# Score products of a quantised attention on 32 rows instead of 128, for the second and third of each four

## The chip, the cores and the metric

The kernel runs on one core of a Trainium2 chip. Its time is in device microseconds (us), the median over several runs; a second figure, the span, goes from the first to the last instruction of one profiled execution. The engines are named as in the profile: PE (TensorE, matrix products; PEld is its weight load, which can lie under a product), DVE (VectorE), ACT (ScalarE), POOL (GpSimd) and SP (SyncE, which here starts the DMAs).

## The reference, cut to what matters

Six layers follow one another on a tensor x of 2 x 128 x 256: a cross attention with 2048 context rows per batch, a mixing layer, experts, a second cross attention with fake quantisation, a dilated attention and a feed-forward layer. The change lies in the fourth. Its 16 heads have 16 dimensions each; all 2 x 128 queries attend all 2 x 2048 keys:

```python
q = _fq_sym(q, axis=-1)
k = _fq_sym(k, axis=-1)
v = _fq_sym(v, axis=2)
attn = jnp.einsum('bhqd,bhkd->bhqk', q, k)
attn = jax.nn.softmax(attn.astype(jnp.float32), axis=-1)
attn = _fq_unsigned(attn, axis=-1)
out = jnp.einsum('bhqk,bhkd->bhqd', attn, v)
```

`_fq_sym` rounds to 127 steps of the largest absolute value, `_fq_unsigned` to 255 steps of the largest. So a row of scores must be known up to its maximum before its exponentials are rounded.

## The kernel before

The program is written by hand, engine by engine, with semaphores; nothing is scheduled for it. The order of each engine is the order of its code.

The quantised attention has 32 units u, one per batch b (0, 1) and head h (0 to 15). A unit has 128 queries and 4096 keys. Its scores are computed twice: a first pass, `pe_first`, in products n of 512 keys (`NB` = 8 per unit, 256 in all), of which DVE takes only the maximum (`dve_first`, tile tops, L1892); and a second pass, `pe_second`, in chunks q of 1024 keys (`NC` = 4 per unit), two products each, of which ACT makes the exponentials (`act_exponentials`, L1885, which writes into the tile that the trace calls cT). SP turns these by DMA (L1980), and PE multiplies them with the values (`attend`, L1908, 16 products of 16 columns after the first two chunks of each unit). All score products are recorded with line 1843, in `pe_scores`, and the trace calls their operands kT and v_space (qT lies in that space).

Four heads share a group of 128 rows: the rows of kT hold, for each group, 4 x 32 rows, 32 per head (16 dimensions in two parts). The queries of one head stand in `m.qT[:, b, group, r, :]`, where r = h mod 4; only rows 32r to 32r + 31 hold them, the other 96 are zeros that POOL writes beforehand.

A slot is one (u, q) of the loop in `pe_attention`: the two second-pass products of chunk q, then two first-pass products for a unit that lies one or two further on, then whatever the side program has due (small stages of the other layers for the other batch), and `attend`. For u = 1 to 31 there are 124 slots; the last six have no first-pass products left. First-pass products use PSUM banks 0, 1, 2 in turn (n % 3), and a product waits until DVE has read the bank (q_max). Second-pass products use banks 3 to 6 in two pairs and wait for ACT (q_exp). The first 20 first-pass products and the four chunks of unit 0 are issued earlier, by `drain` in `pe_cross`, between the products of the last units of the first cross attention (L1060, L1085, L1095, L1098, L1075, L1106, L1112):

```python
DRAIN = (0, 2, 2, 2, 3, 3, 2, 2, 1, 1, 1, 1)
SECONDS = ((1, 1), (1, 2), (2, 0), (2, 2))
```

DRAIN is the number of first-pass products at each of twelve places, SECONDS the places after whose first-pass products a chunk of unit 0 follows. In order, the runs of score products there are: maxima 0 and 1; 2 and 3; 4 and 5; 6 to 8; 9 to 11 with chunk 0; 12 and 13 with chunk 1; 14 and 15; 16, chunk 2 and 17; 18; chunk 3; 19.

One other product matters below: the experts' bias (L1712, fp32), of the 8 rows of `m.coefT` with `m.expert_b`, once per batch.

Of the kernel before, what the change touches and what calls it, by code (L numbers as in the profile page):

```python
# [19 lines left out]
P = 128  # L20
# [39 lines left out]
BLK = 512  # L60
NB = KT * P // BLK
CHUNK = 1024
# [10 lines left out]
DG, DW = 4, 32  # L73
# [946 lines left out]
def pe_cross(pe, m, c, d, g, s, side):  # L1020
# [44 lines left out]
    def drain(u, q):  # L1065
        for n in first_scores_due(u, q):
            pe_first(pe, m, s, n)
        if (n := second_scores_due(u, q)) is not None:
            pe_second(pe, m, s, 0, n)
# [768 lines left out]

def pe_scores(pe, m, u, ps, at):
    b, group, r = u // H1, u % H1 // KG, u % KG
    return pe.matmul(ps, m.qT[:, b, group, r, :], m.kT[:, group, at:at + BLK], start=True, stop=True)  # L1843


def pe_first(pe, m, s, n):

    if n == 0:
        pe.wait_ge(s["exp"], UNITS)
    if n % NB == 0 and n // NB % H1 < KG:  # L1850
        pe.wait_ge(s[f"qu_act{n // (NB * H1)}"], QU_ACT[f"qT{n // NB % H1}"])
    if n > 2:
        pe.wait_ge(s["q_max"], n - 2)
    pe_scores(pe, m, n // NB, m.bank(n % 3), n % NB * BLK).then_inc(s["q_first"], 1)


def second_place(u, q):

    return 3 + 2 * (q % 2) if u > 0 else 3


def pe_second(pe, m, s, u, q):

    n = NC * u + q
    if u == 0 and q > 0:
        pe.wait_ge(s["q_exp"], q)
    elif n == NC:
        pe.wait_ge(s["q_exp"], NC)
    elif n > NC:
        pe.wait_ge(s["q_exp"], n - 1)  # L1870
    if n == NC + 1:
        pe.wait_ge(s["added"], UNITS)
    for k in range(CHUNK // BLK):
        ins = pe_scores(pe, m, u, m.bank(second_place(u, q) + k), q * CHUNK + k * BLK)
    ins.then_inc(s["q_second"], 1)


# [18 lines left out]
def pe_attention(pe, m, x, s, side):  # L1896
# [35 lines left out]
    for u in range(1, UNITS + 2):  # L1932
        for q in range(NC):
            if u < UNITS:
                pe_second(pe, m, s, u, q)
            for n in range(AHEAD + NB * u + 2 * q, AHEAD + NB * u + 2 * q + 2):
                if n < NB * UNITS:
                    pe_first(pe, m, s, n)
            if q == 0:
                side.upto(NC * u - 0.5)  # L1940
            if u >= UNITS and q < 2:
                for n in range(NB // 4 * (2 * (u - UNITS) + q), NB // 4 * (2 * (u - UNITS) + q + 1)):
                    turn(n)
            if u > 1 and q < 2:
                attend(u - 2, q)
            if q > 0:
                side.upto(NC * u + q)
# [691 lines left out]
```

## Time and profile before

| | us |
|---|---|
| median of 3 runs | 688.63 (687.92 to 689.13) |
| span of the profiled execution | 687.7 |
| PE busy | 651.0 (95%) |
| DVE busy | 576.4 (84%) |
| ACT busy | 417.5 (61%) |
| POOL busy | 389.1 (57%) |

The profiled execution has no time of its own besides its span; the runs' median lies 0.9 us above that span. A row of a group of instructions gives line, engine, operation, what it writes and reads, rows and columns of the weights, rows and columns of the moving operand, and the count. Products are pipelined: a product of 512 columns is shown with a length of 379 ns, though the next one may start 216 ns after it, so starts are to be compared, not lengths.

### The profile page before, as it was taken

Reading aid. Unit: us, or ns where it says so; the run is one execution under the profiler, and the core shown is the slowest. Engines: PE = TensorE matmul, PEld = TensorE weight load, DVE = VectorE, ACT = ScalarE, POOL = GpSimd, SP = SyncE. Lnnn points to the kernel's source line nnn. Section 1 sums busy time; section 2 is a strip of 40 time slices with the busy share of each in tenths; the row PEclk is TensorE's granted clock in tenths of the full one; section 3 lists DMA queues with packets and bytes.
Section 4 is the critical chain, followed back from the end, with each engine's and each line's share of the span. In section 5 each row is a group of like instructions: output and inputs, shape, how many; then the busy total and the mean of one; then the engine's idle time right before and its main releaser. Section 6 shows DMA issues by size and latency. Waiting matters only on the chain.

```text
span 687.7 us, 13890 instructions
## 1 busy us (share of the span) xinstructions
PE 651.0 (95%) x5088; PEld 410.1 (60%) x5088; DVE 576.4 (84%) x1029; ACT 417.5 (61%) x697; POOL 389.1 (57%) x500
## 2 busy tenths in 40 slices
PE   8899999999999999999999999999889889988887
PEld 6456766666666676766766666654436444544453
DVE  5998987887897797899989769888877889999655
ACT  5644454444544465565654445549878899899941
POOL 5876666566557736689965516526635543345401
PEclk9999999999999999999999999999989999999999
DMA  9666689765756588988974965639998899999900
GB/s 309 164 147 140 146 184 172 173 140 122 158 122 151 120 196 215 210 173 193 184 168 118 226 144 115 148 81 218 235 186 153 168 149 198 160 185 163 201 14 9
DMA packets 347827, 111.01 MB, mean 161 GB/s; under 512 B 313704, under 2 KB 344432, under 8 KB 347760
## 3 DMA queue, kind: packets, MB, share of 16 engines
q1 hardware_dynamic: 347760, 110.13, 77.1%
q8 instruction: 41, 0.67, 0.4%
q14 instruction: 26, 0.21, 0.1%
HBM read 31.97 MB, written 0.26 MB: 47 GB/s over the span
## 4 chain that ended last, share of the span: by engine, by line
PE 67%; DVE 21%; ACT 5%; issue 3%; DMA 2%; POOL 1%; DVEq 0%; ACTq 0%; POOLq 0%
PE psum L1060 21%; PE psum L1032 20%; DVE tops L1892 8%; PE psum L1843 6%; PE psum L1046 5%; PE psum L506 3%; ACT cT L1885 3%; DVE neg_max L1272 2%; PE psum L1908 2%; DMA c_nat<-cT 2%; PE psum L1085 1%; PE psum L1095 1%; PE psum L827 1%; PE psum L845 1%; DVE e_lo L1260 1%
## 5 line engine op out<-in xcount | busy, mean ns | idle before, releaser
L1060 PE MATMUL psum<-c_nat,eT 128*128 128x256 f16 x1536 | 188.1, 273 | 0.9 <-ACT u_sb L1234 0.9
L1892 DVE TENSOR_REDUCE tops<-psum 128x1 f32<-128x512 f32 x256 | 159.6, 683 | 20.7 <-PE psum L1843 20.1
L1885 ACT ACTIVATE cT<-psum,bias,q_scale 128x1024 f16<-128x1024 f32 x128 | 153.5, 1204 | 22.6 <-PE psum L1843 21.1
L1032 PE MATMUL psum<-cT,qk 128*128 128x512 f16 x744 | 165.6, 379 | 0.1
L1060 PEld LDWEIGHTS psum<-c_nat,eT 128*128 128x128 f16 x1536 | 147.3, 98 | 24.1 <-issue 1.6
L1843 PE MATMUL psum<-kT,v_space 128*128 128x512 f16 x512 | 140.4, 389 | 9.4 <-DVE tops L1892 7.3
L1032 PEld LDWEIGHTS psum<-cT,qk 128*128 128x128 f16 x744 | 72.6, 98 | 82.3 <-issue 1.2
L1272 DVE TENSOR_REDUCE neg_max<-psum 128x1 f32<-128x2048 f32 x32 | 73.2, 2287 | 21.3 <-PE psum L1032 21.2
L1260 DVE TENSOR_TENSOR e_lo<-e_all,e_hi 128x2048 f16<-128x2048 f32 x32 | 88.5, 2767 | 0.0
L1843 PEld LDWEIGHTS psum<-kT,v_space 128*128 128x128 f16 x512 | 45.4, 99 | 71.4 <-DVE tops L1892 34.4
L1203 ACT ACTIVATE e_all<-psum,neg_max 128x2048 f32<-128x2048 f32 x32 | 63.1, 1970 | 16.5 <-DVE neg_max L1274 16.4
L858 ACT ACTIVATE qT<-psum 128x128 f32<-128x128 f32 x31 | 8.6, 279 | 100.8 <-PE psum L827 91.2
L776 POOL TENSOR_TENSOR k_full<-k_int,k_scale 128x256 f32<-128x256 bf16 x32 | 26.7, 836 | 72.1 <-issue 46.9
L1208 ACT CAST e_hi<-e_all 128x2048 f16<-128x2048 f32 x32 | 60.8, 1898 | 1.6 <-DMA eT<-e_hi 0.6
L2012 POOL TENSOR_SCALAR least<-least,tops 128x1 f32<-128x1 f32 x64 | 23.1, 361 | 51.5 <-DVE tops L1892 50.5
L1046 PE MATMUL psum<-wkv,cT 128*128 128x512 f16 x192 | 46.7, 379 | 2.5 <-DVE k_tmp L1326 2.5
L1908 PEld LDWEIGHTS psum<-v_space,c_nat 128*128 128x128 f16 x1024 | 33.9, 96 | 22.4 <-DMA c_nat<-cT 6.4
L746 POOL TENSOR_TENSOR u_parts<-u_sb,u_parts 128x256 f16<-128x256 f32 x30 | 31.7, 1056 | 21.8 <-ACT u_parts L1239 21.7
L1908 PE MATMUL psum<-v_space,c_nat 128*128 128x16 f16 x1024 | 35.4, 170 | 8.3 <-DMA c_nat<-cT 4.0
L777 POOL TENSOR_TENSOR k_parts<-k_int,k_scale 128x256 f16<-128x256 bf16 x32 | 40.9, 1278 | 0.0
L749 POOL TENSOR_TENSOR wvo_parts<-wvo_h,wvo_parts 128x512 f16<-128x512 f32 x30 | 36.7, 1222 | 0.0
L759 POOL TENSOR_TENSOR wqk_parts<-wqk_h,wqk_parts 128x512 f16<-128x512 f32 (+1 forms) x27 | 31.7, 1175 | 0.3
(286 smaller groups left out, 947.3 us busy)
## 6 DMA issues: line engine op xcount, KB each, us to landing
wvo_h<-in_L_xattn_Wv SPq DMA_DIRECT2D x30, 128.0 KB, 2.4
wvo_h<-in_L_xattn_Wo SPq DMA_DIRECT2D x30, 128.0 KB, 2.3
wqk_h<-in_L_xattn_Wq SPq DMA_DIRECT2D x28, 128.0 KB, 2.4
wqk_h<-in_wkT SPq DMA_DIRECT2D x28, 128.0 KB, 2.6
mx_land<-in_mx_weights SPq DMA_DIRECT2D x8, 384.0 KB, 4.0
v_space<-in_ctx SPq DMA_DIRECT2D x4, 512.0 KB, 5.8
cT<-in_ctx SPq DMA_DIRECT2D x2, 1024.0 KB, 8.3
c_nat<-in_expert_wT SPq DMA_DIRECT2D x2, 1024.0 KB, 6.6
```

What stands on the lines that cost most here:

```text
L777: pool.tensor_tensor(hi, ints, scale, ALU.mult).then_inc(s["k_cut"], 1)
L1032: ins = pe.matmul(s_ps[:, n * 512:(n + 1) * 512], c.qk[:, u % 2, q_part, k, :], m.cT[:, b, c_part, 4 * n:4 * n + 4, k, :], start=(k, q_par ...
L1046: ins = pe.matmul(kv_ps, m.cT[:, kt // KTB, c_part, kt % KTB, k, :], d.wkv[w_part][:, k, :], start=(k, w_part, c_part) == (0, 0, 0), stop= ...
L1060: ins = pe.matmul(u_ps, c.eT[:, v % 2, e_part, j, :], m.c_nat[:, v // H0, c_part, j, :], start=(j, e_part, c_part) == (0, 0, 0), stop=(j, ...
L1203: act.activation(c.e_all[:, :], s_ps, ACT.Exp, bias=c.neg_max[:, u % 2:u % 2 + 1], scale=1.0 / UP, accum_out=c.row_sum[:, u:u + 1]).then_i ...
L1208: act.copy(c.e_hi[:, :], c.e_all[:, :]).then_inc(s["e_hi"], 1)
L1260: dve.tensor_tensor(c.e_lo[:, :], c.e_all[:, :], c.e_hi[:, :], ALU.subtract).then_inc(s["e_lo"], 1)
L1272: dve.tensor_reduce(limit, s_ps, AX.X, ALU.max, negate=True).then_inc(s["max"], 1)
L1843: return pe.matmul(ps, m.qT[:, b, group, r, :], m.kT[:, group, at:at + BLK], start=True, stop=True)
L1885: act.activation(m.y[:, u % 2, q * CHUNK:(q + 1) * CHUNK], m.bank(second_place(u, q), 2), ACT.Exp, bias=m.bias[:, u:u + 1], scale=m.q_scal ...
L1892: dve.tensor_reduce(m.tops[:, n // NB, n % NB:n % NB + 1], m.bank(n % 3), AX.X, ALU.max, negate=True).then_inc(s["q_max"], 1)
L1908: ins = pe.matmul(m.bank(7)[:, h * HD1:(h + 1) * HD1], x.yT[:, z % 2, half * KT // NH + j, :], m.v_int[:, half * KT // NH + j, h * HD1:(h ...
```

## The change

`pe_scores` takes a flag. With it, the product reads only the 32 rows of its head, of the queries and of the keys; without it, all 128 rows as before. Since the other 96 rows of the queries are zero, the sum is the same. The flag is set for the second product of each chunk (k == 1) and for the first-pass products with even n. In a slot the order is chunk product 0 (128 rows), chunk product 1 (32 rows), first-pass product of even n (32 rows), first-pass product of odd n (128 rows). The first-pass products of a slot belong to unit u + 1 or u + 2, so the two narrow products have different r and stand on different groups of 32 rows. Order, waits and tiles of all engines stay as they were; only line numbers behind 1841 grow by one.

```diff
--- before.py
+++ after.py
@@ -1838,9 +1838,10 @@
 
 
 
-def pe_scores(pe, m, u, ps, at):
+def pe_scores(pe, m, u, ps, at, own_rows):
     b, group, r = u // H1, u % H1 // KG, u % KG
-    return pe.matmul(ps, m.qT[:, b, group, r, :], m.kT[:, group, at:at + BLK], start=True, stop=True)
+    rows = slice(r * DW, (r + 1) * DW) if own_rows else slice(0, P)
+    return pe.matmul(ps, m.qT[rows, b, group, r, :], m.kT[rows, group, at:at + BLK], start=True, stop=True)
 
 
 def pe_first(pe, m, s, n):
@@ -1851,7 +1852,7 @@
         pe.wait_ge(s[f"qu_act{n // (NB * H1)}"], QU_ACT[f"qT{n // NB % H1}"])
     if n > 2:
         pe.wait_ge(s["q_max"], n - 2)
-    pe_scores(pe, m, n // NB, m.bank(n % 3), n % NB * BLK).then_inc(s["q_first"], 1)
+    pe_scores(pe, m, n // NB, m.bank(n % 3), n % NB * BLK, n % 2 == 0).then_inc(s["q_first"], 1)
 
 
 def second_place(u, q):
@@ -1871,7 +1872,7 @@
     if n == NC + 1:
         pe.wait_ge(s["added"], UNITS)
     for k in range(CHUNK // BLK):
-        ins = pe_scores(pe, m, u, m.bank(second_place(u, q) + k), q * CHUNK + k * BLK)
+        ins = pe_scores(pe, m, u, m.bank(second_place(u, q) + k), q * CHUNK + k * BLK, k == 1)
     ins.then_inc(s["q_second"], 1)
```

## Rows read from the trace of the kernel before

**Rows 1.** The page: span, busy time of each engine

```profile
span 687.7 us, 13890 instructions
PE 651.0 (95%) x5088; PEld 410.1 (60%) x5088; DVE 576.4 (84%) x1029; ACT 417.5 (61%) x697; POOL 389.1 (57%) x500
```

**Rows 2.** The chain that ended last, 463 to 654 us, shares by line

```profile
by line: DVE tops L1892 28.2%; PE psum L1843 19.9%; ACT cT L1885 9.6%; PE psum L1908 6.2%; DMA c_nat<-cT 5.5%; issue 5.2%; PE psum L506 4.5%; POOL xn L464 1.3%; ACT v_space L1812 0.9%; DVE stats L442 0.8%; DVE mx_amax L2234 0.8%; PE psum L2
```

**Rows 3.** Windows: stretch, length, busy time per engine, granted clock, DMA

```profile
core 0: us, PE busy (x) PEld busy (x) DVE busy (x) ACT busy (x) POOL busy (x), PEclk, DMA share, GB/s
442.00:459.00 17.00, 16.13 (x121) 11.70 (x119) 13.87 (x26) 5.52 (x12) 6.99 (x12) 1.00 0.39 92
463.00:654.00 191.00, 170.92 (x1595) 87.79 (x1594) 164.09 (x312) 169.62 (x299) 92.07 (x213) 0.97 1.01 183
465.60:468.60 3.00, 2.25 (x9) 0.62 (x9) 2.97 (x7) 2.87 (x7) 2.00 (x7) 1.00 0.98 241
503.00:511.00 8.00, 7.60 (x67) 3.75 (x68) 4.95 (x10) 4.79 (x7) 2.97 (x6) 0.59 1.14 227
```

**Rows 4.** Timeline of PE, first and last slots of the first kind

```profile
469.13 1.02 PE L1843 MATMUL psum<-kT,v_space 128*128 128x512 f16 x4
469.99 0.17 PE L1908 MATMUL psum<-v_space,c_nat 128*128 128x16 f16 x1
...
643.84 0.55 PE L1908 MATMUL psum<-v_space,c_nat 128*128 128x16 f16 x16
644.24 1.02 PE L1843 MATMUL psum<-kT,v_space 128*128 128x512 f16 x4
```

**Rows 5.** Timeline of PE, 519 to 523 us and about 571 us

```profile
519.70 1.03 PE L1843 MATMUL psum<-kT,v_space 128*128 128x512 f16 x4
520.56 1.03 PE L506 MATMUL psum<-expert_wT,xnT 128*128 128x256 f32 x4
521.42 1.03 PE L1843 MATMUL psum<-kT,v_space 128*128 128x512 f16 x4
522.29 0.55 PE L1908 MATMUL psum<-v_space,c_nat 128*128 128x16 f16 x16
...
570.26 0.81 PE L1843 MATMUL psum<-kT,v_space 128*128 128x512 f16 x3
571.23 0.39 PE L1843 MATMUL psum<-kT,v_space 128*128 128x512 f16 x1 [0.16 <-DVE tops L1892]
```

**Rows 6.** Timeline of PE, 503 to 509 us

```profile
503.40 0.60 PE L1908 MATMUL psum<-v_space,c_nat 128*128 128x16 f16 x16 [2.43 <-DMA c_nat<-cT]
503.85 5.28 PE L1843 MATMUL psum<-kT,v_space 128*128 128x512 f16 x12
```

**Rows 7.** Timeline of PE, the product of 8 rows, both batches

```profile
408.34 0.27 PE L1060 MATMUL psum<-c_nat,eT 128*128 128x256 f16 x1
408.54 0.69 PE L1712 MATMUL psum<-v_abs,coefT 8*128 8x256 f32 x2
...
408.86 0.37 PE L1712 MATMUL psum<-v_abs,coefT 8*128 8x256 f32 x1
409.17 0.23 PE L1085 MATMUL psum<-uT_parts,wvo_parts 128*128 128x128 f16 x1
...
537.75 0.37 PE L1712 MATMUL psum<-v_abs,coefT 8*128 8x256 f32 x1
538.06 0.60 PE L1843 MATMUL psum<-kT,v_space 128*128 128x512 f16 x2
```

**Rows 8.** Waits, 463 to 654 us: total, times, longest

```profile
DVE tops L1892 <- PE psum L1843: 17.0, 26, 3.3
ACT cT L1885 <- PE psum L1843: 16.0, 25, 3.0
```

**Rows 9.** Timeline of PE, 442 to 461 us

```profile
442.71 1.47 PE L1060 MATMUL psum<-c_nat,eT 128*128 128x256 f16 x12
444.02 0.59 PE L1843 MATMUL psum<-kT,v_space 128*128 128x512 f16 x2
...
446.91 1.47 PE L1060 MATMUL psum<-c_nat,eT 128*128 128x256 f16 x12 [0.22 <-ACT u_sb L1234]
...
456.78 0.59 PE L1843 MATMUL psum<-kT,v_space 128*128 128x512 f16 x2
457.21 0.59 PE L1112 MATMUL psum<-wqk_h,oT_parts 128*128 128x256 f32 x2
457.65 1.03 PE L1843 MATMUL psum<-kT,v_space 128*128 128x512 f16 x4
...
459.85 0.60 PE L1843 MATMUL psum<-kT,v_space 128*128 128x512 f16 x2 [0.26 <-ACT cT L1885]
```

**Rows 10.** Timeline of ACT, about 648 us

```profile
648.21 1.20 ACT L1885 ACTIVATE cT<-psum,bias,q_scale 128x1024 f16<-128x1024 f32 x1 [0.37 <-PE psum L1843]
```

## The prediction

> **What bounds the kernel now.** I read the page first: 687.7 us of span, and TensorE (PE) busy for 95% of it [rows 1]. That share does not say where PE decides, so next came the chain that ended last, for the stretch in which the quantised attention runs (463 to 654 us). VectorE's (DVE's) maxima hold 28.2% of that chain, the score products (L1843) 19.9%, ScalarE's (ACT's) exponentials 9.6% [rows 2]. The three engines are busy 171, 164 and 170 us of 191 there [rows 3]: none has much to spare, and they take turns in deciding. In the 17 us before it (442 to 459) PE alone decides: 16.1 us busy, against 13.9 and 5.5 [rows 3].
>
> The reader should see three kinds of slot. I sorted the 124 slots of units 1 to 31 by the starts of their products. In 72 all four products start 215 to 216 ns apart, as in the rows from 469.13 (the first that stands alone) to 644.24 us (the last): four take 1.02 us, and the last start-to-end is 0.38, so 0.216 from start to start and 0.864 for a slot [rows 4, 5]. 33 of these 72 follow sixteen attention products of 25 ns (16 in 0.55 us, 0.17 of it the last one's own length), the others mostly small stages such as the experts' products [rows 4, 5]. In 36 the third or fourth product waits for a DVE maximum, as at 571.23 us [rows 5]. Five run at half clock (427 ns per product, granted clock 0.59 over 503 to 511) [rows 3, 6], four begin late, one has a slow second product, six at the end have no first-pass products. Of the chain's 191 us, 19.9% is 38.0 us, or the products of 44 slots: so much of this is on the path that sets the end.
>
> **The change part by part.** Nothing is moved: each engine issues the same instructions in the same order with the same waits. Of a slot's four products the second and third read 32 of 128 rows instead of all. A product's time goes by its 512 columns, so each alone costs the same 0.216. What can change is (a) whether the second and third run at the same time, on their two row groups, and (b) what it costs to go from a product of 128 rows to one of 32 and back.
>
> (b) has a near row. The experts' bias product (L1712) is the only one of before with few rows: 8. Its first half starts 0.20 us after the last L1060 product, where one L1060 follows another in 0.109 (twelve from 442.71 to 444.02 [rows 9]): 0.09 to go in. Its second half starts at 408.86 and the next full product at 409.17, 0.31 later, where 256 columns of fp32 take 0.215 (four from 520.56 to 521.42 [rows 5]): 0.09 to come out [rows 4, 7]. The other pair, at 537, comes out in 0.31 as well (537.75 to 538.06) [rows 7]. In each case the weight load begins only when the array is empty; a full product loads its weights under the product ahead of it. The one after that starts 10 ns late too (226 instead of 216 ns, as after other idle times: the two at 459.85 take 0.60, those at 456.78 take 0.59 [rows 9]). So in 93, out 91, then 10: about 0.2 us for a lone product of few rows. The Trainium skill (TensorEngine Tiling (Array Packing), Key Properties) says that a change of tiling mode, not of tile, drains the engine; the trace agrees with 0.09 us each way.
>
> (a) has no row: no two products of before stand on different row groups. Bounds: the third starts with the second (0), or 0.216 after it. The nearest row is the attention products, whose weight load and product of 16 columns follow each other in 25 ns [rows 5]; I take 25 ns. The Trainium skill (TensorE: Matmul & The Clock Gate, Measured speedup vs the span model) gives about 4 ns per tile and a 3.07-fold gain for four tiles; no row here shows it, and with 4 ns each slot below would be 21 ns shorter.
>
> A slot with all four ready: first to second 216 + 93 = 309, second to third 25, third to fourth 216 + 91 = 307, fourth to next 226: 867 ns against 864. What the overlap gives back (191 ns) the two drains and the late load take (194). With the third's own load exposed, 877. Over the 44 slots on the path: +0.1 to +0.6 us, I take **+0.3**. The scores for ACT come 0.1 later than now and those for DVE 0.1 earlier; ACT waited for score products 25 times, DVE 26 times [rows 8], so these cancel roughly.
>
> The 36 slots that wait for DVE: the way out falls into the wait before the fourth product (0.16 us of idle at 571.23) or the next slot's, and DVE sets the pace: 0. Without that cover it would be 0.1 each, 3.6 in all.
>
> The five slots at half clock: 427 is saved; the drains are between 0.18 and twice that, and the start 0.025 to 0.05. That leaves 0.01 to 0.2 gained per slot; I take 0.1, **-0.5**.
>
> Before the attention, during the last cross units, the score products of unit 0 and the first 20 maxima stand in ones to fives between full products of other lines [rows 9]. There the same rule (even number, or second of a pair) makes 14 of 28 products narrow, and none has a narrow neighbour on another row group: each pays 0.2 and gains nothing. By rows: one each at 442.28, 444.02, 446.09, two each at 448.21, 451.56 and 454.17, one at 456.78, two at 457.65, one at 459.21, one at 459.85. The one at 446.09 falls into the 0.22 us that PE idles for ACT's u_sb; the one at 459.21 falls into the wait for ACT's exponential; the second at 457.65 counts half (ACT waits for its end, nothing for its way out). The rest is on the path: 11.5 x 0.2 = **+2.3**.
>
> The last six slots have one narrow product each and no partner. ACT waits for a score product at 648.21 us (0.37 idle) [rows 10]; a second product that ends 0.1 later counts in about three of them: **+0.3**; 0 to 1.2 are the bounds.
>
> Sum: 0.3 - 0.5 + 2.3 + 0.3 = +2.4. The profiled span 687.7 becomes 690.1; the runs' median, 688.63, lies 0.9 above that span, so **691.0 us**.
>
> **The rivals.**
> 1. No overlap: the third product waits for the second (its semaphore wait, its load, or the write into PSUM holds it). Then a slot is 309 + 226 + 307 + 226 = 1068, +204 ns. For: no row shows two at once. Against: only the page above, and that nothing in the kernel makes them share a bank. With 44 slots: 9.0 + 2.3 + 0.3 = +11.6, 700 us; if all 72 fast slots come to count, +17.3, 706 us.
> 2. No drain, and overlap (the one that ends faster): the 0.09 us belongs to fp32 or to this product's own operands, not to its few rows. For: L1712 is fp32, the scores are fp16. Against: full fp32 products (L506) follow and precede score products at 0.216 with no such gap [rows 5], and both directions show 0.09. It decides once the two ways together cost under 0.19. A slot saves 0.19; behind attention products only 0.05, as 0.40 + 0.86 = 1.26 falls to the 1.21 of ACT's exponential [rows 4, 10]. 44/72 of (39 x 0.19 + 33 x 0.05) = 5.5: 683 us; with all 72 slots 9.1: 679.5. The TensorE page's span model, which names no drain, would have it so.
> 3. The clock: half-filled products count as less work and the granted clock falls more often. A cold stretch like 503 to 509 (twelve products in 5.28 us instead of 2.75 [rows 6]) costs 2.5 us; two more would give 696. For: the clock fell after 2.4 us of waiting. Against: it stayed at 1.00 through 465.6 to 468.6, where PE waited for DVE and was busy for 2.25 of 3.00 us [rows 3].
> 4. Nothing happens: the rows are masked but the array is used as before, no drain and no overlap. 688.6.
>
> **How the numbers follow.** Drain and overlap 0.60, with its own range 689.3 to 693.0; no overlap 0.17; no drain 0.15; clock 0.04; nothing 0.04. The range must leave out at most 2 in 10: 683.5 leaves out the lower half of the no-drain case (0.07), 702 the upper part of the no-overlap case (0.06). Within 0.2% (1.4 us, about what a measurement tells from no change) is 687.25 to 690.0: the slack that the cross units may find, a quarter of the first case, 0.15, with the fourth and a rest of the second, 0.21. Faster: 0.13 of the second and 0.05 from the first (DVE's earlier scores worth more than ACT's later ones), 0.18. Slower: 0.40 from the first, the no-overlap case 0.17, the clock 0.04, 0.61.
>
> **What would show it.** After: score products of 32 rows; a fast slot with starts 309, about 25, 307, 226 apart; in the cross stretch 442 to 459, score products that start 0.31 apart and the L1112 product near 461.25 some 2 us later; from there the difference stays nearly constant to the end. If second and third stand 226 apart, rival 1; if first and second stand 216 to 230 apart, rival 2. The prediction is wrong too if the attention stretch (191 us) shrinks or grows by over 2 us with these gaps as forecast: then the order of arrivals at DVE and ACT matters more than the sum of PE's time.

## The result, and the profile after

The changed kernel takes 706.82 us (median of 4 runs, 705.19 to 709.43) against 688.27 (687.74 to 689.13): the ratio is 1.0269, with a 95% interval of 1.0245 to 1.0294. It is 18.5 us slower; the forecast was 691.0, 2.7 us slower, with a range up to 702. Where a kernel below has a run that lies over 1.5% above its fastest, its ratio leaves that run out while its median keeps it; this concerns one run of four with the attention alone changed, and three of four with both narrow products on one row group, which has no ratio.

The page of the changed kernel, first the span and the busy times, then the granted clock and the DMA share in 40 slices, then two of the costliest groups:

```profile
span 703.9 us, 13890 instructions
PE 675.4 (96%) x5088; PEld 406.3 (58%) x5088; DVE 579.2 (82%) x1029; ACT 420.1 (60%) x697; POOL 389.0 (55%) x500
PEclk9999999999999999999999999988799788859999
DMA  9566789667656699889776867469999699889910
L1893 DVE TENSOR_REDUCE tops<-psum 128x1 f32<-128x512 f32 x256 | 160.7, 681 | 32.0 <-PE psum L1844 31.9
L1886 ACT ACTIVATE cT<-psum,bias,q_scale 128x1024 f16<-128x1024 f32 x128 | 153.8, 1205 | 34.2 <-PE psum L1844 31.2
```

The busy share of PE says as little as before [rows 1]; DVE and ACT do the same work as before, but over the whole span they now sit idle ahead of these two groups for 32 and 31 us until score products come. The line that tells the story is the granted clock, in tenths: in the last third it falls. Over the whole span it is:

```profile
core 0: 703.9 us, clock 0.949
```

against 0.993 before. In the trace each stretch stands at either 1.00 or 0.50, so (1 - 0.949) x 2 x 703.9 gives the time at half clock: 72 us, where before had 10. The windows of the changed kernel, with the columns of [rows 3]:

```profile
442.00:459.00 17.00, 16.63 (x116) 10.50 (x114) 12.86 (x22) 5.22 (x12) 7.08 (x10) 1.00 0.39 91
463.00:672.00 209.00, 195.82 (x1652) 86.55 (x1653) 169.35 (x319) 174.19 (x304) 93.18 (x214) 0.83 0.93 168
471.50:481.00 9.50, 9.50 (x57) 3.82 (x56) 6.02 (x10) 6.30 (x13) 5.02 (x10) 0.50 1.11 214
484.00:494.00 10.00, 9.47 (x85) 3.98 (x83) 8.81 (x15) 9.34 (x19) 6.94 (x16) 1.00 1.08 184
612.00:634.00 22.00, 22.00 (x153) 7.10 (x152) 16.89 (x32) 16.62 (x29) 8.21 (x23) 0.50 0.78 145
```

The attention now takes 209 us at a mean clock of 0.83, where it took 191 at 0.97 [rows 3]. The falls are not spread thin: stretches such as 471.5 to 481 and 612 to 634 run at 0.50 throughout (1.2 GHz), those between at 1.00 (2.4 GHz). The old kernel fell twice, each time at a long wait of PE: one of 2.43 us for a DMA [rows 6], and one of 1.55 us for ACT shortly before 557.4. The changed kernel falls seven times, at 471.1, 495.0, 518.9, 542.8, 563.3, 587.2 and 611.1 us. The fall at 563.3 comes inside the same wait for ACT, now 1.63 us; the full-clock stretches ahead of the six others hold no wait of PE longer than 0.6 us. The two waits, first before, then after:

```profile
556.11 0.56 PE L1908 MATMUL psum<-v_space,c_nat 128*128 128x16 f16 x16 [1.55 <-ACT v_space L1812]
563.39 0.59 PE L1909 MATMUL psum<-v_space,c_nat 128*128 128x16 f16 x16 [1.63 <-ACT v_space L1812]
```
The chain that ended last, 463 to 672 us, by line:

```profile
by line: PE psum L1844 37.9%; DVE tops L1893 22.3%; PE psum L1909 7.0%; PE psum L506 7.0%; ACT cT L1886 4.3%; issue 2.9%; PE psum L499 1.0%; DVE stats L442 1.0%; DVE c_nat L1970 0.9%; ACT v_space L1812 0.8%; PE psum L2448 0.8%; POOL xn L464
```

The score products went from 19.9% of it [rows 2] to 37.9%, the experts' products (L506) from 4.5% of 191 us (8.6) to 7.0% of 209 (14.6): more of the chain goes to products that the change doesn't touch.

And yet in a slot at full clock all went nearly as forecast. Three narrow windows of the timeline of PE, 489.1 to 489.9 us, part a fast slot into its products:

```profile
489.12 0.38 PE L1844 MATMUL psum<-kT,v_space 128*128 128x512 f16 x1
489.43 0.39 PE L1844 MATMUL psum<-kT,v_space 32*128 32x512 f16 x2
489.75 0.39 PE L1844 MATMUL psum<-kT,v_space 128*128 128x512 f16 x1
```

The first starts at 489.12, the two narrow ones at 489.43, and the two together end 0.39 us later, as one alone would: they run at the same time. In the nanoseconds of the records the starts are 309, 3 and 318 apart; over the 80 slots at full clock the medians are 312, 3, 317 and 227, in sum 859. The Trainium skill (TensorE: Matmul & The Clock Gate, Measured speedup vs the span model) gives about 4 ns per tile; the trace agrees with 3. A slot at half clock, the four products and the attention products behind them:

```profile
622.45 1.67 PE L1844 MATMUL psum<-kT,v_space 128*128 128x512 f16 x4
623.91 0.62 PE L1909 MATMUL psum<-v_space,c_nat 128*128 128x16 f16 x16
```

That is 1.46 us from the slot's start to the attention products instead of 0.86.

### The profile page after: what moved, and what is told of

Read it like the earlier page. It is cut to its first block, busy times and chain, and to the rows that moved or that the text cites. A ratio compares the mean times of both kernels' runs of the same rounds, so it can differ in the third digit from the quotient of the medians.

```text
span 703.9 us, 13890 instructions
## 1 busy us (share of the span) xinstructions
PE 675.4 (96%) x5088; PEld 406.3 (58%) x5088; DVE 579.2 (82%) x1029; ACT 420.1 (60%) x697; POOL 389.0 (55%) x500
## 4 chain that ended last, share of the span: by engine, by line
PE 75%; DVE 18%; ACT 3%; issue 3%; POOL 1%; DVEq 0%; ACTq 0%; POOLq 0%
PE psum L1060 21%; PE psum L1032 20%; PE psum L1844 12%; DVE tops L1893 7%; PE psum L1046 5%; PE psum L506 3%; PE psum L1909 2%; DVE neg_max L1272 2%; ACT cT L1886 1%; PE psum L1085 1%; PE psum L1095 1%; PE psum L827 1%; PE psum L845 1%; DVE e_lo L1260 1%; PE psum L890 1%
## 5 line engine op out<-in xcount | busy, mean ns | idle before, releaser
L1844 PE MATMUL psum<-kT,v_space 128*128 128x512 f16 (+1 forms) x512 | 158.9, 445 | 8.0 <-DVE tops L1893 4.5
L1844 PEld LDWEIGHTS psum<-kT,v_space 128*128 128x128 f16 (+1 forms) x512 | 39.4, 98 | 106.2 <-issue 68.2
L776 POOL TENSOR_TENSOR k_full<-k_int,k_scale 128x256 f32<-128x256 bf16 x32 | 24.1, 755 | 72.6 <-issue 52.3
L1909 PEld LDWEIGHTS psum<-v_space,c_nat 128*128 128x128 f16 x1024 | 35.5, 99 | 16.2 <-issue 5.7
L777 POOL TENSOR_TENSOR k_parts<-k_int,k_scale 128x256 f16<-128x256 bf16 x32 | 44.7, 1396 | 0.0
L2011 POOL TENSOR_SCALAR least<-tops 128x1 f32<-128x1 f32 x32 | 12.2, 381 | 42.4 <-DVE tops L1893 42.3
```

The lines of the kernel that those rows point to most:

```text
L777: pool.tensor_tensor(hi, ints, scale, ALU.mult).then_inc(s["k_cut"], 1)
L1844: return pe.matmul(ps, m.qT[rows, b, group, r, :], m.kT[rows, group, at:at + BLK], start=True, stop=True)
L1909: ins = pe.matmul(m.bank(7)[:, h * HD1:(h + 1) * HD1], x.yT[:, z % 2, half * KT // NH + j, :], m.v_int[:, half * KT // NH + j, h * HD1:(h ...
```

## The experiments

**Which theory of the clock.** Theory A: it goes by how many of the array's rows are at work. Theory B, the rival: it goes by how long the array streams at all, which the overlap shortens. The first run makes only one product of a slot narrow, the second keeps both but puts them on one row group.

```diff
-        ins = pe_scores(pe, m, u, m.bank(second_place(u, q) + k), q * CHUNK + k * BLK, k == 1)
+        ins = pe_scores(pe, m, u, m.bank(second_place(u, q) + k), q * CHUNK + k * BLK, False)
```

> Narrow are only the first-pass products with even n; both chunk products stay at 128 rows, so nothing overlaps. Both theories: in a fast slot the starts are 216, 309, 307 to 318, 226 apart, some 0.2 us more per slot, which on the 44 to 72 slots that count gives +9 to +15 us, and +2 in the cross units. Theory A (the granted clock follows how many of the array's rows are at work): one product of four at a quarter of the rows, so the clock falls too, but less than with two; mean clock 0.95 to 0.98, time 703 to 715. Theory B (the clock follows the time in which the array streams at all, which the overlap shortened by a quarter): nothing overlaps here, mean clock 0.985 or more, time 698 to 705.

Measured: 705.0 us (ratio 1.0208, 1.0171 to 1.0245), granted clock 0.980 to 0.993 over the four runs. A fast slot has starts 216, 312, 317, 226 ns apart: nothing overlaps. Three runs have a clock of 0.98, lower than the 0.993 to 1.000 of before though nothing overlaps, and higher than with two narrow products; the fourth (0.993, 700.4 us) fits theory B as well. So this run leans to A and doesn't decide.

```diff
-    rows = slice(r * DW, (r + 1) * DW) if own_rows else slice(0, P)
+    rows = slice(0, DW) if own_rows else slice(0, P)
```

> The two narrow products read rows 0 to 31, whatever their head (the scores of three heads in four are then wrong, their maxima and exponentials too), so both stand on one row group. Both theories: no overlap, second and third 216 to 226 apart, a fast slot of about 1068 ns, +12 to +17 us by that alone. Theory A: two products of four at a quarter of the rows, clock as low as in the changed kernel or lower (0.95 or less), time 712 to 730. Theory B: the array streams all the time, clock 0.985 or more, time 699 to 706.

Measured: 779.3 us (754.0 to 787.7). Even the fastest run, with the clock at 0.891, is slower than either theory said. The profiled run's clock and a window of its attention:

```profile
core 0: 773.2 us, clock 0.856
473.00:554.00 81.00, 81.00 (x404) 28.02 (x404) 42.72 (x78) 45.25 (x78) 25.83 (x59) 0.50 0.72 134
```

81 us on end at 0.50, with PE shown busy for all 81. The drains count as busy there: a slot at half clock is 566, 400, 562, 398 ns, 1926 in all, of which four products of 427 are 89%. So with no overlap, and with the array streaming for some nine tenths of such a slot (an estimate from these starts), the clock is far below the changed kernel's: theory B, with its 0.985, falls. Whether the rows or the drains do it is left open here and taken up again below. A fast slot is 312, 226, 307, 226; the prediction's first rival had worked out 309, 226, 307, 226 for products that don't overlap.

The converse, less streaming at full rows:

```diff
+    cols = 64 if n >= sum(DRAIN) and n % 2 == 0 else BLK
-    pe_scores(pe, m, n // NB, m.bank(n % 3), n % NB * BLK).then_inc(s["q_first"], 1)
+    pe_scores(pe, m, n // NB, m.bank(n % 3), n % NB * BLK, cols).then_inc(s["q_first"], 1)
```

> The kernel before, all products at 128 rows, but in the attention the first-pass products of even n have 64 columns instead of 512 (their maxima are then taken over stale scores). So the array streams for as many columns per slot as with the overlap (3.1 products instead of 4), at full rows and without drains. Theory A: clock as before (0.98 or more), slots up to 0.19 us shorter, 676 to 684 us. Theory B: clock as in the changed kernel (0.94 to 0.96), and the lost clock eats the gain: 690 to 700 us.

Measured: 687.38 us (ratio 0.9982, 0.9971 to 0.9993), clock 0.985 to 0.993, in the middle 0.988 against 0.995. The clock nearly holds, as theory A has it, and is nowhere near B's 0.94 to 0.96. But the time lies outside both expectations: the four products of a slot take 0.19 us less (0.84, below, against 1.03 in [rows 5]) and the kernel gains 1.4 us of 688.8. The chain of this kernel has DVE's maxima at 29.5% and the DMA at 8.3%, where before had 28.2% and 5.5% [rows 2].

```profile
525.62 0.84 PE L1843 MATMUL psum<-kT,v_space 128*128 128x512 f16 x4
526.35 1.13 PE L506 MATMUL psum<-expert_wT,xnT 128*128 128x256 f32 x4
527.32 0.84 PE L1843 MATMUL psum<-kT,v_space 128*128 128x512 f16 x4
by line: DVE tops L1893 29.5%; PE psum L1843 15.8%; ACT cT L1886 10.5%; DMA c_nat<-cT 8.3%; PE psum L1909 5.8%; issue 5.6%; PE psum L506 5.2%; POOL xn L464 1.3%; ACT v_space L1812 0.9%; DVE stats L442 0.8%; DVE mx_amax L2235 0.8%; PE psum L
```

The 0.19 is not free time for PE, though. From one slot with experts' products to the next it is 1.70 us here and 1.72 before [rows 5]: the products behind the short one take back nearly all of it. Over the 59 slots that run at full clock and without a wait in both kernels, the time from one slot's start to the next is 0.09 us shorter in the mean. So 1.4 us is what this shortening brought, at a clock a little lower than before; it is no bound on what a third product that costs nothing could bring.

**A version with no drains inside a slot.** All four products narrow, the order chunk 0, first-pass even, chunk 1, first-pass odd:

```diff
+        if k == 0 and between is not None:
+            pe_first(pe, m, s, between)
...
-                if n < NB * UNITS:
+                if n < NB * UNITS and (n % 2 or u >= UNITS):
```

> All four score products of a slot of the attention are narrow, in the order chunk 0, first-pass even, chunk 1, first-pass odd, so that two pairs overlap and no drain lies between the four; in the cross units all stay at 128 rows. Both theories: starts 4, 216, 4 apart at full clock, the four in about 0.43 us instead of 0.86, with one drain in and one out. Theory A: the clock is half through nearly all of the attention (mean clock 0.85 to 0.90); the pairs take 427 each, a slot about as long as before, but the side stages in fp32 and bf16 double: 688 to 705 us. Theory B: the array streams half as long, the clock is low as well; the same numbers. If the clock stays full, TensorE no longer bounds the attention and the time falls to 665 to 680.

Measured: 715.93 us (ratio 1.0374, 1.0331 to 1.0418), clock 0.846 in the profiled run. Nearly the whole attention is at half clock, as theory A (and B) had it, but the time is 11 us above the upper bound of 705: a slot has 3, 397, 5, 561 ns, 966 in the median, where two pairs of 427 would make 854.

```profile
463.00:688.00 225.00, 211.18 (x1610) 82.71 (x1607) 166.96 (x313) 175.08 (x300) 92.83 (x213) 0.51 0.84 156
```

**The terms outside the attention.** Only the 14 lone products ahead of it, then all but them (each by the condition n < sum(DRAIN) and u == 0, or its opposite):

> Narrow are only the 14 lone products ahead of the attention; the attention's own are as before. Prediction's step: 11.5 of them on the path at 0.2 us, +2.3 us (690.5 to 691.5). If the attention finds slack for a late start: +0.5 to +1.5. Clock as before (0.99) by both theories, since the wide products around them keep the array busy.

> The changed kernel with the 14 products ahead of the attention back at 128 rows. If costs add: 706.8 less the 2.6 us of the run with those alone, 704 us, clock 0.94 to 0.96; the attention's narrow pairs then carry 15 to 16 us by themselves.

Measured: 691.29 us (ratio 1.0045, 1.0029 to 1.0061), clock 0.993 to 0.998, so +2.6 by the medians and +3.1 by the ratio; and 704.42 us (1.0167, 1.0093 to 1.0242), clock 0.933 to 0.966. The medians add up to the change's 18.5 (2.6 and 16.2), but the runs of the second scatter from 695.6 to 710.1 with their clock, so this is no close check.

**64 rows instead of 32.** Two products on the two halves of a group fill the array while they overlap. This works in the 88 slots in which the heads stand on different halves:

```diff
+def apart(u, q):
+    v = (AHEAD + NB * u + 2 * q) // NB
+    return 0 < u and v < UNITS and u % KG // 2 != v % KG // 2
...
+    rows = slice(r // 2 * 2 * DW, (r // 2 + 1) * 2 * DW) if own_rows else slice(0, P)
```

> The second and third product of a slot of the attention have 64 rows (their own half of the group; the other 32 are zeros), in the three slots of four in which the two stand on different halves; all else has 128 rows, in the cross units too. Starts about 310, 4, 316, 226 apart as with 32 rows. Theory A: while the two overlap, all 128 rows are at work, so the clock stays at 0.98 or more and the time at 686 to 691. If it is not rows but the narrow mode, the drains or the overlap itself that lower the clock: 0.94 to 0.96, 698 to 708 us.

Measured: 690.20 us (ratio 1.0024, 1.0011 to 1.0037), clock 0.985 to 0.993. Slots in the trace have starts 311, 3, 319, 227 apart, as with 32 rows. The clock nearly holds: 0.990 in the mean of the runs, before 0.997. The same with all four narrow, two overlapping pairs:

> All four products of a slot with 64 rows, in the order chunk 0, first-pass even, chunk 1, first-pass odd, in the three slots of four in which the halves differ; two pairs overlap, 0.43 instead of 0.86 us at full clock, one drain in and one out per slot: 0.24 us less of TensorE's time per slot than before. Theory A: rows at work times time is half of before in these slots while the engine idles more; if that lowers the clock (0.90 to 0.96) the time is 690 to 705; if not, 683 to 688, since the slots with a short third product showed how little a faster TensorE is worth at full clock (1.4 us for 0.19 per slot).

Measured: 697.21 us (ratio 1.0115, 1.0093 to 1.0136), clock 0.954 to 0.963. The first of the two cases expected: PE is busy for fewer of the microseconds (93% of the span, before 95%), and the clock falls after all.

**Work that makes it faster.** A product of 128 rows whose result is overwritten, ahead of each slot's first, in the changed kernel, in the one before, and in the one with a lone narrow product:

```diff
+    if u > 0:
+        pe_idle_product(pe, m, m.bank(second_place(u, q)))
     for k in range(CHUNK // BLK):
```

> The changed kernel with one more product of 128 rows and 512 columns ahead of each slot's first (into the PSUM bank that the first then overwrites): 124 x 0.216 = 27 us of work more, of which by the 44 to 72 slots that count 10 to 15 us would lie on the path. Theory A: the wide product brings the clock back to 0.985 or more; the 16 us go, the filler's come: 697 to 704 us, not slower than the changed kernel although it does more. If the clock does not come back: 717 us or more.

> The kernel before with the same filler product ahead of each slot's first. It is the base for the filled changed kernel (700.0 us). If overlap and drains cancel at full clock, as the fast slots say (858 against 863 ns), and all else of the 18 us was clock: 696.5 to 698 us, that is 700.0 less the 2.6 us of the cross units and next to nothing for the attention. If the attention's order of arrivals costs something by itself: below 695.

> Only the first-pass products of even n narrow, with the filler. It prices a lone narrow product at full clock: 0.21 us in each of 118 slots and 2 in the cross units. By the share of slots on the path (44 to 72): 9 to 15 us over the kernel before with filler, 708 to 714; if the waits in the attention hide much of it, as they hid the short third product's gain: 700 to 705. Clock 0.99 or more.

Measured: 699.99 us (ratio 1.0170, 1.0149 to 1.0191) for the changed kernel, 6.8 less than without the extra 124 products; 697.29 (1.0135, 1.0110 to 1.0160) for the one before; 710.39 (1.0328, 1.0295 to 1.0360) with one lone narrow product. The clocks and the attention's window, in this order:

```profile
core 0: 697.8 us, clock 1.000
463.00:665.00 202.00, 192.16 (x1752) 85.81 (x1753) 168.25 (x317) 174.03 (x305) 92.72 (x214) 1.00 0.96 174
```

```profile
core 0: 695.3 us, clock 0.998
463.00:663.00 200.00, 190.88 (x1759) 101.69 (x1760) 167.78 (x316) 172.80 (x302) 92.37 (x213) 0.99 0.97 175
```

```profile
core 0: 708.3 us, clock 1.000
463.00:675.00 212.00, 207.91 (x1744) 95.14 (x1743) 170.11 (x315) 177.82 (x302) 92.77 (x214) 1.00 0.89 165
```

At one and the same clock the change costs 699.99 - 697.29 = 2.7 us (2.4 by the ratios), and the cross units alone cost 2.6. So the overlap and the drains of the attention cancel, to within the 2 us that the two intervals leave. By subtraction the rest of the 18.5, about 15.8 us, is the clock: 62 us more at half speed cost about a quarter of their length. The four runs of the changed kernel say nearly the same without a filler: from clock 0.949 to 0.935, 20 us more at half clock, their time goes from 705.2 to 709.4, a fifth. An estimate from this slope puts the changed kernel at some 691 us if its clock stood at 0.997.

The lone narrow product costs 13.1 us at full clock, for 0.21 in each of 118 slots and in 10 places of the cross units; 710.4 lies in the higher of the two expected ranges. The filler itself cost the kernel before 9.0 us, as 42 products of 0.216 would: near the 44 slots that the prediction had counted as on the path.

**Rows, or narrow mode and drains as such?** The 64-row kernel has wide slots too. So its twin with 32 rows in the same 88 slots:

> The kernel with 64 rows (690.2 us, clock 0.988), with 32 instead of 64 rows in the very same 88 slots; overlap, drains, order and all wide products the same. Theory A (rows at work): clock 0.94 to 0.97, 696 to 706 us. If instead the 64-row kernel kept its clock because only three slots in four were narrow: clock 0.985 or more and 689 to 692 us.

Measured: 693.46 us (689.85 to 695.15; ratio 1.0084, 1.0057 to 1.0112), clock 0.975 to 0.993. Both expectations miss: 3.3 us more than with 64 rows (ratio 1.0011 to 1.0037), but far less than with all slots narrow (704.4). The number of rows counts, for nothing else differs between the two kernels and their intervals lie apart; the share of wide slots counts more. The profiled run was the fastest, at 0.993, so the fall itself stands in the clocks of the other runs alone. A third theory, C, was therefore still open: that drains and narrow mode lower the clock whatever the rows. The run with both products on one group, again, with 64 rows:

```diff
-    rows = slice(r * DW, (r + 1) * DW) if own_rows else slice(0, P)
+    rows = slice(0, 2 * DW) if own_rows else slice(0, P)
```

> As the run in which both narrow products read rows 0 to 31 (clock 0.86, 754 to 788 us), but rows 0 to 63, so that nothing but the number of rows differs, in all slots: no overlap, starts about 312, 226, 307, 226 apart, the same drains (scores of two heads in four are wrong). Theory A (rows at work): the clock is far higher, 0.94 or more, and the time 704 to 735 us. Theory C (drains and the narrow mode as such, whatever the rows, let the clock fall; the 64-row kernel was spared by its wide slots): clock 0.84 to 0.90, 750 to 790 us.

Measured: 715.12 us (712.98 to 721.69; ratio 1.0416, 1.0362 to 1.047), and in the profile:

```profile
core 0: 711.7 us, clock 0.969
463.00:677.00 214.00, 203.21 (x1596) 82.00 (x1595) 167.65 (x314) 173.27 (x300) 92.30 (x213) 0.90 0.89 162
```

The slots are the same to 2 ns (311, 226, 309, 226 against 312, 226, 307, 226), the drains too; 64 rows instead of 32 bring the clock of the profiled run from 0.856 to 0.969 and the time from 779 to 715 (fastest against fastest 754 to 713). So C cannot be the whole cause, and the number of rows is a large part of it. That drains and narrow mode have a part too is not excluded: 0.969 is still below 0.993. One more difference stands between these two runs. In rows 0 to 31 the queries of three heads in four are zeros, in rows 0 to 63 those of two in four, and no run shows whether zeros alter the clock. The pair with 88 narrow slots is free of this, since both of its kernels read each head's own queries; its effect is smaller.

Where this kernel falls says something too. The wait and the stretch behind it, twice:

```profile
506.40 0.56 PE L1909 MATMUL psum<-v_space,c_nat 128*128 128x16 f16 x16 [1.88 <-DMA c_nat<-cT]
507.60:527.90 20.30, 20.30 (x107) 6.81 (x106) 12.55 (x30) 11.48 (x20) 6.06 (x14) 0.50 0.80 147
567.75 0.56 PE L1909 MATMUL psum<-v_space,c_nat 128*128 128x16 f16 x16 [1.53 <-ACT v_space L1812]
569.00:592.80 23.80, 23.80 (x128) 7.31 (x128) 14.99 (x28) 14.84 (x26) 6.76 (x18) 0.50 0.66 122
```

In the attention it falls only at the two long waits at which the kernel before fell, but stays at half clock for 20 and 24 us where that one came back after 7 and 3. The kernel with one lone narrow product does the same (20 and 7 us). With two products of 32 rows, overlapping or on one group, the clock also falls where PE had waited for nothing longer than 0.6 us.

## Why the prediction was wrong

Direction yes, size and cause no: 706.8 lies outside 683.5 to 702, and the likeliest case gave 691. The prediction named a sign of being wrong, an attention that grows by over 2 us with the gaps as forecast, and it came (191 to 209 us). But it would have read it as the order of arrivals at DVE and ACT, and it was the clock.

- The drains were right. Forecast 93 in and 91 out, from a product of 8 rows in fp32; measured 96 in (312 instead of 216) and 101 out (317), and 10 or 11 on the one after. The Trainium skill's rule on a change of tiling mode (TensorEngine Tiling (Array Packing), Key Properties) holds with these numbers.
- The overlap was right in kind and better than the 25 ns taken: 3. A fast slot was forecast at 867 ns and is 859, against 863 before; the prediction said that 4 ns would make it 21 shorter, and drains dearer by 13 took most of that back. Both rivals that stood on this term, no overlap and no drain, are out.
- The term of the cross units was right: forecast +2.3, measured +2.6 (ratio 1.0029 to 1.0061).
- The attention at full clock: forecast +0.3, and +0.3 for its last slots; measured 0.1 in all with the clock held up by the filler, which the runs tell from 0.6 no better than from nothing.
- The 44 slots on the path were a fair count for a cost. The filler cost the kernel before 9.0 us, 42 slots of 0.216. Lone narrow products cost 13.1 us on top of the filler; about 2 of it lies in the cross units (an estimate, 10 of their 14 products), so 11 in the attention: 53 slots of 0.208. For a gain the count is not borne out: the short third product gained 1.4 us, as 16 slots of the 0.09 that it freed would. The clock was a little lower there, and the chain names who came last and does not say how close behind the next one was; which of the two kept the gain small is open.
- **The step that failed is the third rival**, given 0.04. Two things in it were wrong. Its argument against, that the clock stayed at 1.00 from 465.6 to 468.6 with PE busy for 2.25 of 3.00 us [rows 3], was about products of 128 rows, so it spoke of time and not of rows; no row of before had a stretch of narrow products, and this should have widened the bound instead of closing it. And its price was two more cold stretches of 2.5 us; there were 62 us more at half clock, for about 15.8. The forecast also took -0.5 for five cold slots as a gain, where the question was how many there would be: at least 29 lie wholly at half clock, at 1.506 us each.

The Trainium skill (TensorE: Matmul & The Clock Gate, What's actually happening) says that the clock is set by how busy PE has been. The runs here show that busy cannot mean time alone: in both pairs that differ in rows but not in their slots, 64 rows keep more clock than 32 (0.990 against 0.984 in the means of the runs with 88 narrow slots; 0.969 against 0.856 in the profiled runs on one group). What stays open is how the chip weighs the rows, and what part the drains have. The runs order as A says where rows go from 32 to 64 and from one narrow product to two; the filler adds rows at work and takes idle time away at once, so it shows that the clock was lost and not why. And it is no proportion: three slots in four at 32 rows cost about 0.01 of clock (0.984 in the mean of the runs, before 0.997), all of them about 0.05.

No version that computes the same result beats the kernel before. The best, with 64 rows, is 0.24% slower; the short third product, which leaves out part of the work, gave 0.18%.

## What to carry to other kernels

A product on fewer rows can cost clock: before narrowing products in a stretch that lives at full clock, ask how many rows are left at work, and hold the granted clock of a trial beside its time. Overlap on row groups is real (3 ns apart), but each change between full and narrow costs 0.1 us, which makes a lone narrow product a loss of 0.2. To change less often is no way out by itself: the two versions whose slots have no change inside lost more clock (715.9 and 697.2 us). Before an engine is made faster, shorten its work by leaving some out and look at the time, and look also at what the products next to the short one do with the gap: here a small gain of 1.4 us was in sight before anything was built.

## What the runs showed of the hardware that was not expected

- PE busy for 81 us on end at half clock, with two products of four on 32 rows of one group (clock 0.856 over the run); with 64 rows in their place 0.969, and the longest stretch at half clock 24 us.
- Falls of the clock with no wait of PE longer than 0.6 us ahead of them, six of seven in the changed kernel.
- More work, less time: 124 wide products of 0.216 us each took the changed kernel from 706.8 to 700.0 us, its clock from 0.949 to 1.000.
- Two products of 32 rows, or of 64, on different row groups start 3 ns apart and take the time of one, at either clock; at half clock the way in costs 0.14 (567 instead of 427 ns), the way out 0.11 (537), and the four products 1.506 us where four wide ones of 427 ns take 1.708.
- The scatter between runs grows with the share of half clock: 1.4 us of 688 before, 4 us of 707 after, 34 us with both products on one row group.
